# Reordering the start of a mixture-of-experts stage: where statistics, loads, logits and first transposes stand

## The reference, cut to what matters

```python
# x: 10000 x 512, 5000 edges sorted by destination, 2 relations
h   = relu(rgcn(layernorm(x), layer 1))       # rgcn: per relation, gate * x[col] @ w_r, summed by row,
out = rgcn(h, layer 2)                        # plus x @ root + bias
x   = x + out
t   = layernorm(x)
shared = gelu(t @ sw1 + sb1) @ sw2 + sb2.sum(0)          # 2 shared experts, 64 hidden each
probs  = softmax(t @ gate_w.T + gate_b); top 2 of 8
routed = sum over the two: prob * (gelu(t @ rw1[e] + rb1[e]) @ rw2[e] + rb2[e])
x = x + shared + routed
```

## Time and profile before

| | us |
|---|---|
| median of three runs | 1618.26 |
| lowest and highest | 1615.1, 1620.84 |
| profiled execution, device time | 1620.96 |
| its span in the trace | 1619.2 |
| PE busy | 1488.7 |
| DVE busy | 929.4 |
| ACT busy | 708.1 |
| POOL busy | 657.6 |

### The profile page before, as it was taken

The page is one execution under the profiler, slowest core; times in us unless marked ns, Lnnn a source line. Parts: engine busy times, 40 slices in busy tenths (PEclk is TensorE's granted clock), DMA queues, the critical chain, the costliest instruction groups (busy, mean ns, idle before and its releaser), DMA issues. The chain is left out here.

```text
span 1619.2 us, 27768 instructions
## 1 busy us (share of the span) xinstructions
PE 1488.7 (92%) x8680; PEld 1201.8 (74%) x8680; DVE 929.4 (57%) x2667; ACT 708.1 (44%) x1230; POOL 657.6 (41%) x989
## 2 busy tenths in 40 slices
PE   6999988988998999999999985699999999999997
PEld 5776666777786677767888863588787878888886
DVE  5555676857752333334766477567566666665453
ACT  3333334656642112222666436355564646453222
POOL 3762232457753000000566535555545464543222
PEclk9999999999999999999999998799999999999999
DMA  9999999697757999998677697888757676533220
GB/s 240 280 278 289 294 291 290 192 284 125 129 86 182 304 280 286 278 283 242 163 131 131 94 247 180 234 210 251 213 187 198 200 202 190 165 126 131 92 73 4
DMA packets 130212, 325.95 MB, mean 201 GB/s; under 512 B 17115, under 2 KB 17641, under 8 KB 129698
## 3 DMA queue, kind: packets, MB, share of 16 engines
q1 hardware_dynamic: 84626, 211.19, 44.2%
q0 software_dynamic: 45456, 113.12, 30.9%
HBM read 205.62 MB, written 121.74 MB: 202 GB/s over the span
## 5 line engine op out<-in xcount | busy, mean ns | idle before, releaser
L1201 ACT ACTIVATE th<-bank 128x512 fp32r<-128x512 f32 x158 | 94.4, 598 | 290.6 <-PE bank L1471 290.4
L999 POOL DMA_INDIRECT gx<-y,dst_slot x42 | 44.8, 1067 | 267.2 <-ACT xn_e L1221 245.7
L1820 DVE SCALAR_TENSOR_TENSOR tl<-bank,th 128x512 fp32r<-128x512 f32 x79 | 54.5, 690 | 169.9 <-ACT th L1201 169.7
L1133 POOL DMA_INDIRECT out<-xt,out_row x90 | 94.4, 1049 | 132.0 <-DVE xt L2176 95.4
L1451 PE MATMUL bank<-root2h,th 128*128 128x512 f32 x316 | 132.6, 420 | 12.3 <-DVE tl L1820 6.2
L1451 PE MATMUL bank<-root1h,th 128*128 128x512 f32 x316 | 132.0, 418 | 10.7 <-DVE yout L1847 7.1
L1847 DVE TENSOR_TENSOR yout<-bank,bias_b 128x512 f32<-128x512 f32 x150 | 102.4, 683 | 41.3 <-DMA y<-yout 20.8
L1451 PE MATMUL bank<-root2l,th 128*128 128x512 f32 x316 | 126.0, 399 | 0.0
L1451 PE MATMUL bank<-root1l,th 128*128 128x512 f32 x316 | 125.2, 396 | 0.0
L1451 PE MATMUL bank<-root2h,tl 128*128 128x512 f32 x316 | 125.1, 396 | 0.0
L1451 PE MATMUL bank<-root1h,tl 128*128 128x512 f32 x316 | 125.0, 396 | 0.0
(11 more groups left out here) (353 smaller groups left out, 4380.8 us busy)
## 6 DMA issues: line engine op xcount, KB each, us to landing
basis_t<-in_gnn_basis SPq DMA_DIRECT2D x64, 896.0 KB
xt<-sorted_rows SPq DMA_DIRECT2D x45, 560.0 KB, 3.9
xin<-in_x SPq DMA_DIRECT2D x39, 512.0 KB, 9.6
xin<-y SPq DMA_DIRECT2D x39, 512.0 KB, 7.9
y<-yout SPq DMA_DIRECT2D x37, 512.0 KB, 9.4
z<-yout SPq DMA_DIRECT2D x34, 512.0 KB, 7.9
stage0q<-in_x SPq DMA_DIRECT2D x5, 1024.0 KB, 7.7
stage1q<-in_x SPq DMA_DIRECT2D x5, 1024.0 KB, 8.2
```

Source lines behind the costliest of these rows:

```text
L999: pool.indirect_dma_start(out=gx[:, e % 6, :], out_offset=None, in_=x if pr.phase == SB else y1, in_offset=bass.IndirectOffsetOnAxis(ap=ds ...
L1133: pool.indirect_dma_start(out=out, in_=xt[i % 4][:, j, 0:H], in_offset=None, out_offset=bass.IndirectOffsetOnAxis(ap=out_row[:, i % 4, j:j ...
L1201: act.activation(th_a[:, s, :], tpb[s][:], f).then_inc(s_hi, 1)
L1820: ins = dve.scalar_tensor_tensor(out=tl_a[:, s, :], in0=tpb[s][:], scalar=0.0, in1=th_a[:, s, :].bitcast(F32), op0=ALU.max, op1=ALU.subtract)
```

## The change

It moves work without adding or removing arithmetic:

- SP loads the rows of `x` of groups 0 and 1 inside phase D, as soon as the gather buffers below them are free, and groups 2 and 3 at the start of late C. The stage buffers change places for that.
- In late C, the statistics of groups 0 and 1 stand one step earlier on DVE. Four of the 14 weight pieces move into the lead (`E_SPLITS`).
- In the lead, ACT, PE and DVE take the groups in another order. Groups 1 and 3 have a bank of their own for logits (`logit_bank`). PE transposes tile 0 ahead of group 4. POOL sorts groups 0, 1 and 2 in a row, ahead of `add_z(5)`.
- In the slots, DVE's `q_stats(q_more)` stands behind `routed_lo` and no longer ahead of the register loads and `weigh`; and each half of `turn_hidden` waits for its own half of `weigh`.

```diff
-        stage = (stage0q, stage1q, stage2q, stage3q, stage4q)
+        stage = (stage1q, stage2q, stage0q, stage3q, stage4q)
...
+        E_SPLITS, SPLITS = 5, FC + 1 + 8
...
+        def logit_bank(q):
+            return bank[1] if q in (1, 3) else bank[7]
...
+            sp.wait_ge(s_xn, 2 * ET)
+            load_group(0)
+            sp.wait_ge(s_el, 2 * ET)
+            load_group(1)
             sp.wait_ge(s_mm, E0)
             load_up_experts()
-            load_group(0)
-            load_group(1)
+            load_group(2)
             for g in range(NC // 2 + 4, NG + 1):
                 sp.wait_ge(s_tp, Step(SE, Pos(2 * (g - 4) + 1)).T.k + 1)
                 load_pair(SE, Pos(g))
-                load_group(g - NC // 2 - 2)
+                if g < NG:
+                    load_group(3)
...
             sort_rows(0)
+            sort_rows(1)
+            sort_rows(2)
+            add_z(5)
             group_rstd(4)
             group_extras(4)
-            sort_rows(1)
-            add_z(5)
-            sort_rows(2)
+            sort_rows(3)
             group_rstd(5)
-            sort_rows(3)
             add_z(6)
...
             def turn_hidden(i):
-                pe.wait_ge(s_gs, 2 * i + 2)
                 wait_turn_bank(pe, "g", i)
                 b = turn_bank("g", i)
                 for c, j in itertools.product(range(2), range(2)):
+                    if j == 0:
+                        pe.wait_ge(s_gs, 2 * i + c + 1)
                     ins = pe.transpose(b[:, c * FW + j * P:c * FW + (j + 1) * P], gelr[:, j, c * P:(c + 1) * P], ident[:])
...
+            logits_by_token(2)
+            count_ranks(1)
+            turn_group(3)
+            count_ranks(2)
+            logits(3)
             logits_by_token(3)
-            count_ranks(2)
+            count_ranks(3)
+            for part in ("a", "b", "x"):
+                turn_tile(0, part)
             turn_group(4)
             logits(4)
-            count_ranks(3)
             logits_by_token(4)
-            for part in ("a", "b", "x"):
-                turn_tile(0, part)
...
-                if e == 8:
+                if e == 7:
                     gate_tiles()
                     q_stats(0, range(QT))
-                if e == 9:
+                if e == 8:
                     q_stats(1, range(QT))
...
-                if q_more is not None and q_more > 5:
-                    q_stats(q_more, range(2, QT))
                 chunks = [dve.value_load(pick_int[0:1, i, c:c + 1], min_val=1, max_val=FC - 1) for c in (2, 3)]
                 for c in range(2):
                     weigh(i, c, chunks[c])
...
                 shared_lo(i)
                 routed_lo(i)
+                if q_more is not None and q_more > 5:
+                    q_stats(q_more, range(2, QT))
                 if exists(i + 1):
                     f_lo(i + 1, "a")
                     f_lo(i + 1, "b")
```

More of the change, by code:

```diff
@@ L1343, in q_logits @@
                 wait(act, s_lgx, q)
-                act.activation(lgt[:, 0:n], bank[7][:, 0:n], ACT.Identity, bias=gbias[:, 0:1]).then_inc(s_lgt, 1)
+                act.activation(lgt[:, 0:n], logit_bank(q)[:, 0:n], ACT.Identity, bias=gbias[:, 0:1]).then_inc(s_lgt, 1)
             def q_exp(q):
@@ L1389, in _ @@
                     expert_hi(i)
-                if i >= 2:
+                if 2 <= i < 2 + E_SPLITS:
                     expert_hi(FC + i - 2)
@@ L1394, in _ @@
                 q_full(0, k)
[L1395 to L1402, removed]
+            q_norm(1)
+            q_logits(0)
+            for k in range(KC):
+                q_full(1, k)
+            q_norm(2, range(2))
+            q_exp(0)
+            q_norm(2, range(2, QT))
+            q_logits(1)
+            for k in range(KC):
+                q_full(2, k)
+            q_exp(1)
+            q_logits(2)
+            q_norm(3, range(2))
             q_exp(2)
+            q_norm(3, range(2, QT))
+            for k in range(KC):
+                q_full(3, k)
             q_logits(3)
-            q_norm(4, range(2))
+            for n in range(FC + E_SPLITS, SPLITS):
+                expert_hi(n)
             q_exp(3)
-            q_norm(4, range(2, QT))
+            q_norm(4)
+            for part in ("a", "b"):
+                f_hi(0, part)
+            f_shares(0)
             for k in range(KC):
@@ L1410, in _ @@
             q_logits(4)
-            for part in ("a", "b"):
-                f_hi(0, part)
-            f_shares(0)
             q_exp(4)
@@ L1581, in logits @@
                 pe.wait_ge(s_qtf, KC * q + KC)
-                wait(pe, s_l2, q)
+                wait(pe, s_l2, q if q >= LEAD_GROUPS else q - 1)
                 if q >= LEAD_GROUPS:
@@ L1586, in logits @@
                 for k in range(KC):
-                    ins = pe.matmul(bank[7][32 * k:32 * k + 32, 0:n], gwp[:, k, :], tfull[:, k, 0:n],
+                    ins = pe.matmul(logit_bank(q)[32 * k:32 * k + 32, 0:n], gwp[:, k, :], tfull[:, k, 0:n],
                                     start=True, stop=True, tile_position=(0, 32 * k))
@@ L1593, in logits_by_token @@
                 for j in range(tiles_of(q)):
-                    ins = pe.transpose(bank[7][:, j * P:(j + 1) * P], lgt[:, j * P:(j + 1) * P], ident[:])
+                    ins = pe.transpose(logit_bank(q)[:, j * P:(j + 1) * P], lgt[:, j * P:(j + 1) * P], ident[:])
                 ins.then_inc(s_lgx, 1)
@@ L1692, in _ @@
             logits(0)
-            for q in range(1, 4):
+            for q in (1, 2):
                 q_transpose(q, 0)
@@ L2066, in route_a @@
                 dve.wait_ge(s_lgx, q + 1)
-                parts = bank[7][:, 0:n * P].rearrange("p (j k e) -> p j e k", k=KC, e=32)[:, :, 0:NE, :]
+                parts = logit_bank(q)[:, 0:n * P].rearrange("p (j k e) -> p j e k", k=KC, e=32)[:, :, 0:NE, :]
                 link(dve.tensor_reduce(lg[:, 0, 0:n, :], parts, AX_X, ALU.add))
@@ L2185, in _ @@
                     expert_lo(e)
-                if e >= 2:
+                if 2 <= e < 2 + E_SPLITS:
                     expert_lo(FC + e - 2)
@@ L2209, in _ @@
             sort_kinds(1)
-            q_stats(4, range(QT))
             route_a(2)
@@ L2214, in _ @@
             sort_kinds(2)
-            route_a(3)
+            q_stats(4, range(QT))
             positions(2)
             pick_tile(0)
+            route_a(3)
+            for n in range(FC + E_SPLITS, SPLITS):
+                expert_lo(n)
             route_b(3)
             sort_kinds(3)
-            q_stats(5, range(QT))
             positions(3)
@@ L2223, in _ @@
             pick_tile(2)
-            route_a(4)
             for part in ("a", "b"):
                 f_lo(0, part)
+            q_stats(5, range(QT))
+            route_a(4)
             route_b(4)
```

## The result

The changed kernel takes 1605.36 us (median of 7 runs, 1601.33 to 1610.98), the kernel before 1618.26 (7 runs, 1615.03 to 1623.9). The ratio is 0.9918, with a 95% interval of 0.9893 to 0.9942. I had forecast 1600.7 us, in a range of 1591 to 1609. The profiled execution took 1610.98 us, the slowest of the seven, with a span of 1609.2, 10.0 less than that of before.

The account below looks back on a forecast made before the run. PE bounds the slots, waiting for `weigh`; a chain of small steps bounds the lead. 1620.96 - 20.6 (slots) + 3.0 (lead) = 1603.4; the profiled execution lay 2.7 above the median, so 1600.7 us, range 1591 to 1609.

Parts of the forecast that it names:

- (a): Slots: `q_stats(q_more)` behind `routed_lo` lets `weigh` follow the gelu, so the odd slots' gaps vanish; 15.1 us gained.
- The rival that kept half of the gaps: Odd slots: register loads slow for another reason than place, or `route_a` late; half of 15.1 lost, 1608.2 us; chance 0.10.
- (b): Slots: with `turn_hidden` in halves, two transposes run during the second `weigh`; 2.9 us in even slots, 2.6 in last slots.
- Slots in sum, 20.6: All slots: 15.1 from the moved statistics, 2.9 and 2.6 from the halves of `turn_hidden`; 20.6 us gained.
- The wait moved from tile 1 to tile 2: First slots: the 2.94 us wait for tile 1 goes but moves on to tile 2, so it isn't gained.
- Scatters, +0.7: Phase D: early loads cost its scatters about 3.2 us, the last pair's scatter gains 2.5; 0.7 lost in sum.
- Late C, +4.7: Late C: group 1's statistics wait for the rows of `z`, so the last `tl` delays PE's last product by 4.7 us.
- The new order taken as worth 4.7: Lead: the new order of groups gains 4.7 us, between nothing and 7, so `positions(2)` comes when it came, plus 0.7.
- The lead in sum, +3.0: Lead: tile 0 comes at 1025.1, then group 4's 6 us lie open; slot 0 starts 3.0 us later, all lost.
- The margin of 0.15 us for `route_a`: Odd slots: the later `route_a` on DVE still ends 0.15 us before ACT's table load, which covers it.

Follow-up runs that it names:

- e1: Kernel before with one edit: `q_stats(q_more)` stands behind `routed_lo`; 1603.6 us, ratio 0.9911 to the kernel before.
- e5: Kernel before with DVE's two register loads taken ahead of `q_stats(q_more)`, which stays ahead of `weigh`; 1603.64 us, ratio 0.9892.
- e9: Kernel before with one edit on POOL: in a slot, `add_z` stands behind `store_tile`, `rows_of_tile` and `group_rstd`; 1629.19 us, ratio 1.0052.
- e3: Kernel before with both edits of the slots (statistics moved, `turn_hidden` in halves) and nothing of the lead; 1599.59 us, ratio 0.9876.
- e8: Changed kernel with the loads of groups 0 and 1 back in late C; 1604.66 us, ratio 0.9919 to the kernel before.
- e4: Changed kernel with both edits of the slots undone; 1621.05 us, ratio 1.0014 to the kernel before.
- e6: Changed kernel with `gate_tiles` and the statistics of groups 0 and 1 back at steps 8 and 9 of late C; 1602.28 us, ratio 0.9903.
- e7: Changed kernel with tile 0's transposes, on PE and in ACT's copies, back behind group 4; 1602.95 us, ratio 0.9908.

## Why the prediction came out as it did

*The range, the sign and the mechanism of the slots were right; the forecast was 4.7 us too low. The lead's sum came out in the trace partly by luck, from terms that were off and cancelled.* By steps:

- **(a) the statistics moved, 15.1 us**: 16.0 in e1's trace, 14.9 by the medians (1618.45 in its own runs of before). The place was right too: the loads make `weigh` late, not the statistics (e5). I took the register loads as slow behind statistics without asking why they took 1.6 us; statistics ahead don't lengthen them (e9), and all loads of more than 1 us have transfers beside them. The rival that kept half of the gaps had named POOL's transfers. It failed, as far as the traces tell, because the loads of slot 3, once moved, start 0.9 us behind the issue of `add_z` instead of 3.1. That part was luck: the prediction had no row for it.
- **(b) the halves**: the last slots 2.6, measured 2.3. The even slots' 2.9 is the step that failed: nothing of it arrives beside (a). "Four take 0.66 us with overlap, so two free about 0.24" was right for the start of the turn and wrong for the next one.
- **Slots in sum, 20.6**: 18.3 in e3, 17.1 in the changed kernel; these two have equal slots and differ within the 1.3 us by which the column repeats.
- **The wait moved from tile 1 to tile 2**: right, and the clock moved with it, of which the prediction doesn't speak. Behind the 2.25 us wait on tile 2 the mean granted clock was 0.75,

```profile
1063.20:1070.00 6.80, 6.73 (x30) 5.72 (x31) 4.05 (x23) 1.21 (x3) 4.14 (x12) 0.75 0.57 145
```

  and tile 2 to the turn of slot 2 took 14.03 us instead of 12.60, 1.4 more. In the kernel before, the lower clock stood behind the wait on tile 1 (0.74 from 1043.4 to 1050.0), where the changed kernel has 1.00 (1048.5 to 1055.0).
- **Scatters, +0.7**: mechanism right (e8), by the second scatter of a pair; net +0.5 in the changed kernel's trace, -0.7 on the mean of the four kernels with early loads against the ten others.
- **Late C, +4.7**: 4.7 in the trace (two waits for `tl`, 0.97 and 2.57).
- **The new order taken as worth 4.7**: an assumption without a row. Slot 0 began 4.6 us late, not 3.0. Tile 0 came 2.2 us earlier from the marker instead of 3.0: its load was issued 5.1 us earlier, but took 6.49 us instead of the 3.7 of before, a term that the prediction left as it was. From tile 0 to slot 0's first product it took 10.3 us instead of 9.5. DVE has four weight pieces to split here now, 2.49 us, ahead of group 3's shares.
- **The lead in sum, +3.0**: 3.1 in the trace of the changed kernel, 2.7 in e4's median, but 5.8 to 6.8 between e3 and the changed kernel. The 3.1 is made of other terms than mine: slot 0 4.6 late; the wait on tile 1, 2.94, gone and one of 2.25 on tile 2 in its place; 2.2 won from slot 0 to tile 2, where the mean clock was 0.80 and 1.00 in the two slots instead of 0.75 and 0.74; 1.4 lost behind tile 2. If the difference to e3 is taken, the term was too small by about 3 us, which with (b)'s even slots makes up the miss; by e4's median it was right. e6 points to late C for 2 to 3 of it; the rest isn't located, since the lead's own spread is 3.6 us.
- **The margin of 0.15 us for `route_a`** held: PE shows no wait of that kind. In slot 3 of the changed kernel `route_a` ends at 1097.32 and ACT's table load at 1097.55, a margin of 0.23.

## What to carry to other kernels

Where "issue" ends an idle time behind instructions that are short enough, look at the length of the register loads there before moving the instructions: one line that takes the loads ahead (e5, 14.8 us by the medians) was worth as much as the whole move (e1, 14.9). A wait on a tile's load that is taken away comes back at the next tile as long as what sorts or loads that tile hasn't moved; price the chain to the last of them first. And an assumption that a reordering "is worth about what it costs" needs an experiment of its own: here the reordered start, the larger part of the change, gained nothing and, against e3, cost some us, and the two small edits beside it gave all.

## What was not expected of the hardware

- A register load (`TENSOR_LOAD`) took 0.30 us or 1.1 to 1.65 in the kernel before. In all traces together those of more than 1 us had transfers of POOL's queue beside them, mostly with packets of 2 KB; beside larger packets, at a share over 0.9, 152 of 156 took under 0.6. PE's loads vary too, here those for slot 4's tile, issued in slot 3 of the changed kernel:

```profile
L1737 PEldq TENSOR_LOAD <-pick_int x3: 408/887/1398, 1093.3 to 1096.3; - x3
```

  and PE stood 1.23 us at 1097.06 behind them; before, the same three took 0.30, 0.42 and 1.12 and no wait stood behind them. The Trainium skill (DMA: Bandwidth & Descriptors, "Latency and other measured facts") gives such a load a floor of about 600 ns. The traces don't agree: the median of the 90 loads on DVE is 302 ns in the kernel before. The view names PE's idle time "issue", three times, 2.2 us in all in the changed kernel.
- The clock after a wait of nearly the same length wasn't the same. Tile 2's wait of 2.25 us (changed kernel) was followed by a mean of 0.75 and one of 2.19 (e7) by 0.74. Behind one of 2.09 (e6) it stayed at 1.00:

```profile
1057.10:1064.00 6.90, 6.84 (x40) 5.95 (x41) 4.16 (x23) 2.90 (x5) 4.14 (x12) 1.00 0.62 185
```
